# One table of PSUM banks, five slots of probabilities and new engine orders in an attention and mixture-of-experts block

## The reference

```python
xn = layernorm(x)
q, k = rope(xn @ wq), rope(xn @ wk);  v = xn @ wv          # each key head serves four query heads
attn = softmax(where(causal, q @ k.T / sqrt(16), -inf))
top_scores, selected = top_k(xn @ router_w.T, 2);  gate = softmax(top_scores)
h = silu(x1) * x3        # x1, x3: xn in bf16 by the selected experts' w1, w3
out = x + (attn @ v) @ wo + sum over the two experts of gate * (h @ w2)
```

## Time and profile before

| | |
|---|---|
| time, median of 3 runs (lowest to highest) | 286.12 us (286.11 to 286.59) |
| the profiled execution's own time | 285.75 us |
| its span from first to last instruction | 284.0 us |
| PE busy | 259.5 us, 91% of the span |
| DVE, ACT, POOL busy | 225.2, 219.7, 126.0 us (79%, 77%, 44%) |
| chain of work that ended last | PE 64%, DVE 25% (line 662 alone 23%), ACT 4% |
| mean granted TensorE clock | 0.994 of full speed |

### The profile page before, as it was taken

The page is one execution under the profiler, slowest core; times in us unless marked ns, Lnnn a source line. Parts: engine busy times, 40 slices in busy tenths (PEclk is TensorE's granted clock), DMA queues, the critical chain, the costliest instruction groups (busy, mean ns, idle before and its releaser), DMA issues.

```text
span 284.0 us, 6305 instructions
## 1 busy us (share of the span) xinstructions
PE 259.5 (91%) x2307; PEld 113.0 (40%) x2307; DVE 225.2 (79%) x312; ACT 219.7 (77%) x518; POOL 126.0 (44%) x260
## 2 busy tenths in 40 slices
PE   0876599989999999899999998999999999999996
PEld 0433355533343232334443433446523334433454
DVE  3563879899999999998999999995799998033342
ACT  1479867878788888999888887875688878888841
POOL 8366559356439607952136335247004424035020
PEclk9999979999999999999999999999999999999999
DMA  7516384111157003709262001022000300120205
GB/s 240 173 36 121 68 132 112 23 21 21 21 56 113 20 2 75 114 1 133 77 186 42 4 1 40 1 58 62 15 0 18 98 3 0 49 65 18 78 18 166
DMA packets 49102, 17.62 MB, mean 62 GB/s; under 512 B 43120, under 2 KB 48560, under 8 KB 49072
## 3 DMA queue, kind: packets, MB, share of 16 engines
q1 hardware_dynamic: 48384, 16.43, 27.5%
q10 hardware_dynamic: 688, 0.79, 0.8%
...
## 4 chain that ended last, share of the span: by engine, by line
PE 64%; DVE 25%; ACT 4%; issue 3%; POOL 3%; POOLq 0%; ACTq 0%
DVE PM L662 23%; PE ps L814 17%; PE ps L795 10%; PE ps L754 8%; PE ps L780 7%; PE ps L833 6%; PE ps L854 5%; PE ps L823 3%; PE ps L852 3%; PE ps L772 2%; PE ps L744 2%; PE ps L841 2%; ACT PR L548 1%; POOL RSTD L399 1%; ACT MIXED L511 1%
## 5 line engine op out<-in xcount | busy, mean ns | idle before, releaser
L548 ACT ACTIVATE PR<-ps 128x512 f32<-128x512 f32 (+1 forms) x320 | 156.2, 558 | 31.5 <-PE ps L795 29.5
L662 DVE TENSOR_REDUCE PM<-ps 128x8 f32<-128x1024 f32 x144 | 166.7, 1216 | 7.0 <-PE ps L780 6.8
L456 POOL TENSOR_SCALAR_AFFINE_SELECT PR<-PR 128x512 f32<-128x512 f32 x64 | 39.9, 638 | 87.9 <-ACT PR L548 87.9
L814 PE MATMUL ps<-PR,VA 128*32 128x512 f32 (+3 forms) x768 | 78.1, 495 | 0.5 <-ACT OA L555 0.4
L795 PE MATMUL ps<-STACKS 64*128 64x512 f16 (+3 forms) x384 | 72.6, 327 | 1.4 <-ACT PR L548 0.5
L780 PE MATMUL ps<-STACKS 64*128 64x128 f16 (+2 forms) x640 | 59.7, 264 | 5.0 <-DVE PM L662 4.3
L795 PEld LDWEIGHTS ps<-STACKS 64*128 64x128 f16 x384 | 23.3, 93 | 52.2 <-ACT PR L548 37.8
L780 PEld LDWEIGHTS ps<-STACKS 64*128 64x128 f16 x640 | 26.1, 95 | 38.0 <-DVE PM L662 27.3
L471 POOL TENSOR_TENSOR HB<-MIXED,GATE 128x512 bf16<-128x512 f32 x16 | 16.5, 1044 | 29.8 <-DVE MIXED L716 29.0
L754 PE MATMUL ps<-WP,XT 128*128 128x392 f32 x64 | 26.9, 557 | 1.6 <-ACT XT L494 1.6
L814 PEld LDWEIGHTS ps<-PR,VA 128*32 128x32 f32 x768 | 16.9, 108 | 26.4 <-issue 25.3
...
## 6 DMA issues: line engine op xcount, KB each, us to landing
...
STACKS<-MT SPq DMA_DIRECT2D x64, 2.0 KB
...
STACKS<-MIXED SPq DMA_TRANSPOSE x16, 3.8
MT<-MPW SPq DMA_TRANSPOSE x16, 2.5
```

The lines of the kernel that those rows point to most:

```text
L456: mask = g.affine_select(out=blk, in_=blk, compare_op=ALU.is_ge, fill=0.0, base=0, pattern=[[0, GRP], [1, P]], channel_multiplier=-1)
L548: a.activation(PR[:, k % RING, j, 0:width], bank(step)[:, 0:width], ACT.Exp, scale=scale_bits).then_inc(s_exp, 1)
L662: v_.tensor_reduce(spots, two_banks(step).rearrange("p h (a s n) -> p h a s n", a=2, n=P), AX.X, ALU.max).then_inc(m_max, 1)
L814: mm = t_.matmul(o_bank[VW * j:VW * (j + 1), CHUNK - width:CHUNK], VA[:, b * KVH + grp, kb, :], PR[:, n % RING, j, at:at + width], start=i ...
```

## The change

- `RING` is 5 instead of 3: five slots of probabilities.
- The two bank rings and the fixed bank 7 are gone. `BANKS` holds a digit per TensorE step, its first bank out of all eight (a maximum takes that one and the next; "-" takes none). `places_of` looks up which step held the bank last, and `bank_free` waits for that step's reader, whichever engine that is.
- The products of a job accumulate in the bank of the job's first product (`o_bank(o)`), which differs from job to job; the wait for the copy out is now that bank's wait.
- All five strings of `ORDER` are new. No step is added or taken away, and none changes its work.

```diff
-RING = 3
+RING = 5
...
-        "vssyasseessvssEEssvsaevsssyssyssrrssvssvssveavEEryaaayayyy"),
+        "sEysssssseyassssvvssssarvvsssssseEyssssvvvvrErEayaaayayyyy"),
...
-BANKS_V, BANKS_S = 4, 3
-FILLED_V = dict(project=1, maxima=2, untwisted=1, experts=1, factors=1, output=1)
-FILLED_S = dict(turned=1, projected=1, scores=1, flat=1)
+BANKS = (
+    "76-547653642765402705472076527064276046702654075427104613504275407425743072453704265-65046-246703246"
...
+FILLED = dict(range=1, turned=1, project=1, projected=1, maxima=2, scores=1, product=1, untwisted=1, experts=1, factors=1, flat=1, output=1)
...
-    places, held, filled = {}, {}, [0, 0]
-    for step in steps:
+    places, held = {}, {}
+    for step, digit in zip(steps, BANKS):
         places[step] = []
-        for n, (kinds, first, banks) in enumerate(((FILLED_V, 0, BANKS_V), (FILLED_S, BANKS_V, BANKS_S))):
-            width = kinds.get(step[0], 0)
-            if n == 0 and width == 2:
-                filled[n] += filled[n] % 2
-            for at in range(width):
-                bank = first + filled[n] % banks
-                filled[n] += 1
-                places[step].append((bank, held.get(bank)))
-                held[bank] = (step, at)
+        if digit == "-":
+            continue
+        for at in range(FILLED[step[0]]):
+            bank = int(digit) + at
+            places[step].append((bank, held.get(bank)))
+            held[bank] = step
...
-        o_bank = ps[:, 7, :]
+        def o_bank(o):
+            return bank(("product", PRODUCTS.index((o, 0))))
...
-            (kind, n), _ = before
-            after(nc.tensor, READ_OUT[kind], n + 1)
+            kind, n = before
+            after(nc.tensor, READ_OUT[kind], (PRODUCTS[n][0] if kind == "product" else n) + 1)
...
-                    a.copy(OA[:, o % 2], o_bank).then_inc(o_taken, 1)
+                    a.copy(OA[:, o % 2], o_bank(o)).then_inc(o_taken, 1)
...
-                        after(pe, o_taken, o)
+                        bank_free(step)
```

More of the change, by code:

```diff
@@ new lines @@
+        "vmsssmvmsssmsvsmsrmsssmvssmsvmsssvmsssmrsssrmsmvssmsvssmssvmssmvssmvmssmsvsmssvmmsssvssmssmvmssmsssm"
+        "sssmvmssmssvsmsmssvmsssvmsmssrmssvmsmssvsmssmsssssvsssvsssssmvvssmvssmrssrsmssmsmssvmssvmsmssvssmsms"
+        "ssvmssmvmsmssvssmsmsvsmssvmsmssvmsmssvmssvmssmsssmssrssmvmssvmsssrvmssssvssssmsvvemssreasmsssaEssmss"
+        "ssEremsssvmssvmsmsvvssmeEmsssvmsssvmserEysmmssareymssymssmssEavmssmsvssmEaysmsmeymssvvssmssvmssvmsss"
+        "mvssmeaEmssvmsseearyssmssvssssmvEEssmssvsmssvssmssvmsemssssvmsmeEvsmssvmssEeassvvssssssEyeassssvvsss"
@@ new lines @@
+        "sEysssssseyassssvvssssarvvsssssseEyssssvvvvrErEayaaayayyyy"),
+    ACT=(
+        "xxNNNzljxlzxxjNjzjlxlNNxNjNzljjxzzxzlzxxjJzzJxlJzxzJlxssJslssxJsxssssJsssssssssslsssssssvJsssssslsss"
+        "sssvssssssslsssvssssssslssssssvsssssssssssssssssslssssssssvsssssssssssssssslssssssssssssssssssvsssss"
+        "ssssslssssssssssssGsssvsssssssssssssssssssvssssssssssssssvsssssssssvesseassssassssssesssssssvssessss"
+        "sssevssseassssssasssssassessssssssssssvsessaseeasssssssssssssssssssssessssvsesssssesassssssesassssss"
+        "ssssssssessavssssssasssssssssesvaaaaa"),
@@ L290, in two_banks @@
             return ps[:, places[step][0][0]:places[step][0][0] + 2, :]
-        o_bank = ps[:, 7, :]
-        READ_OUT = dict(turned=xb_sb, project=v_taken, projected=v_spread, maxima=m_max, scores=s_exp, untwisted=o_norm,
+        def o_bank(o):
+            return bank(("product", PRODUCTS.index((o, 0))))
+        range_bank = bank(("range", 0))
+        READ_OUT = dict(range=sized, turned=xb_sb, project=v_taken, projected=v_spread, maxima=m_max, scores=s_exp, product=o_taken, untwisted=o_norm,
                         experts=silu, factors=hidden, flat=a_sb, output=y_ready)
@@ L732, in _ @@
                     pe.wait_ge(w_max, 1)
-                    t_.transpose(o_bank[0:1, 0:P], WMAX[:], IDF[:]).then_inc(w_ps, 1)
+                    t_.transpose(range_bank[0:1, 0:P], WMAX[:], IDF[:]).then_inc(w_ps, 1)
                 elif kind == "scales":
@@ L737, in _ @@
                     pe.wait_ge(made, 2)
-                    t_.matmul(o_bank[:, P:P + 1], ONE[:], LARGEST[:], start=True, stop=True).then_inc(w_wide, 1)
+                    t_.matmul(range_bank[:, P:P + 1], ONE[:], LARGEST[:], start=True, stop=True).then_inc(w_wide, 1)
                 elif kind == "turned":
```

36 lines of the change are left out of this document (16 added, 20 removed).

## The result

The changed kernel takes 272.02 us (median of four executions, 271.75 to 272.39), the kernel before 286.12 beside it: a ratio of 0.951, 95% interval 0.949 to 0.953, so it is faster by 14.1 us. The forecast was 281.8, its range 277 to 288. The sign was right, the size less than a third of the real one.

A forecast was written before the change was run, and what follows sets the result against it. VectorE was taken to bound B, TensorE C and D, neither A. Terms 0 (A), −0.7 (B), −0.5 (C), −3.1 (D) sum to −4.3 from 285.75 us: 281.5, forecast 281.8 as the runs' median is 0.37 higher; range 277 to 288.

The forecast's parts named there:

- 0.075 us for each, pause and price together: TensorE in C and D: time beyond counted steps, 8.0 us over 107 changes of kind and 4.5 over 59, per change.
- C: Stage from the 113th maximum to the last, TensorE setting the pace: steps 49.1 us and 109 changes, 57.3, so −0.5 us.
- D: Stage from the last maximum to the last matmul: steps −2.3, sixteen fewer changes −1.2, last job's first score +0.4; −3.1 us.
- The +0.4 for the last job's first score: Stage D: the maxima's way back takes 10.3 us, with some 9.6 us of TensorE's work in between; +0.4 us or so.
- B: Stage from first to 113th maximum, VectorE: rotation +1.0, one `e` and one `E` +1.4, waits −3.1; −0.7 us, bounds +2.4, −4.4.
- 147.5 by my count: TensorE in stage B after the change: steps 125.4 us plus 294 changes at 0.075, against VectorE's 149.0; VectorE still decides.
- A: Stage from first matmul to first maximum: it waits for the fourth tile's stack, whose chain keeps its length; 0, ±1.5 us.
- Banks and slots elsewhere: nothing: All stages: 61 scores now wait for VectorE's banks, products stand further behind scores; costed at nothing.
- Waits go throughout: Rival: wider distances remove a third of pauses in C and D, B loses 6.8 us of waits; 276 us, chance 0.10.
- B gives nothing: Rival: TensorE and VectorE hinder each other, B 2 us longer; D gives only 1.5; 286 us, chance 0.13.
- The first score of a job waits for its rows: Rival: late rows hold TensorE's queue and VectorE runs dry, some 12 us of waits; 290 us, chance 0.14.
- The clock: Rival: the new order opens pauses elsewhere five times and the clock falls to half more often; 290 us, chance 0.03.

The follow-up runs named there:

- e14: After, with stage D's 128-row steps split up behind whole pairs of scores, ScalarE's order there moved along, own bank table: 277.18 us, ratio 0.972 to before.
- e1: Kernel before with five slots of probabilities for three, nothing else changed: 286.09 us, ratio 1.002 to before.
- e6: Kernel before with five slots and a looser fitted table over all eight banks, orders unchanged: 285.70 us, ratio 1.001 to before.
- e2: Orders of before and three slots, with a newly made table over all eight banks: 288.85 us, ratio 1.012 to before.
- e3: Orders of before with a newly made table over all eight banks and also five slots: 288.56 us, ratio 1.010 to before.
- e4: After's orders and five slots with another table over all eight banks, 513 digits different: 283.31 us, ratio 0.989 to before.
- e12: After, with stages C and D rearranged on all engines by a search for fewer waits, table refitted there: 278.19 us, ratio 0.971 to before.

## Why the prediction was wrong in size

*The step that failed* is "0.075 us for each, pause and price together", with the sentence that two stages agree on it. It took two things as one fixed rate per change of kind: a price of 0.10 us, paid only where the array's tile changes shape, and waits. Changes within one shape, 44 of the 107 in C and mostly between maxima and scores, cost nothing; and the product's 0.99 us already held one price, as the row after it was a score. That the two stages agreed was chance: C had 0.10 × 63 + 3.0 of waits, D 0.10 × 47 + 1.2, over products that were each 0.1 too dear, and C was read as 57.8 us where it has 57.1 from the 113th maximum on (7.3 us over 107 changes are 0.068, not 0.075). Since the rate was held constant, no wait could go.

- **C**, forecast −0.5, came to −3.7. The steps were right (−0.7). Changes of kind rise from 107 to 109, but those of shape fall from 63 to 53 (−1.0), and 2.0 us of waits go.
- **D**, forecast −3.1, came to −5.7. The steps were right (−2.3 forecast, −2.1 here). The change term was −1.2 for sixteen; it was −2.6 for 26 changes of shape, and 0.9 of waits went. The +0.4 for the last job's first score did not come in after (in e14 0.38 did).
- **B**, forecast −0.7, came to −2.5. The two terms moved in, 2.4 us, and VectorE as the bound were right: its busy time rises by 2.6 (143.9 to 146.5 us). The waits were undercounted: its idle time falls by 5.1 (6.5 to 1.4), not by 3.1. The clock had no term there, and how much of the 5.1 is its share is open: no execution of before on record has a mean granted clock above 0.994, all four of after read 1.000, and in e1 3.4 us more of low clock went with 1.3 us. That TensorE, at 147.5 by my count, was only 1.5 us away was wrong by the same rate: 140 changes of shape at 0.10 for 294 of kind at 0.075, and 50 products each 0.1 shorter, make some 134.
- **A**, forecast 0, came to −2.1 (−1.4 by the medians of all profiles, within the 1.5 either way). I followed the fourth tile through its engines and left out what happens at 7 to 10 us, where the range step stood behind a tile.
- **"Banks and slots elsewhere: nothing"** holds for before's orders with more slots or a looser table (e1, e6) and for after's own table, but as a condition: a table that doesn't fit loses 3 us with before's orders (e2, e3) and 11 with after's (e4).

*The rivals.* "Waits go throughout", 276 us, was nearest; its argument against itself, that the 0.10 us at a change has no wait in it, was true, and still the waits went as well. "B gives nothing" did not happen. "The first score of a job waits for its rows" exists, in one job and when a transfer lands late: 1.4 us, not 8. The clock did not fall more often in after, and its fall in before went away. By the Trainium skill's rule that was weighed there, "TensorE: Matmul & The Clock Gate", section "A second HAM failure mode: psum-queue depth-cycling", a table over eight banks would have brought falls between two levels; the trace of after reads 1.00 in all four stages. The falls in the other profiles stand in kernels with two rings (before, e1) as with eight banks (e2, e12), nearly all between 27 and 45 us, around the first maxima.

Still open: why e14 and e12 wait more in D, beyond what the trace names; how much of B's gain is the clock's; and what in A, besides the range step, gave the rest.
